# Entering a deformable round of a MetaFormer kernel, ScalarE copies the first image's turned hats before it takes the second image's absolute distances

## The chip, the cores and the metric

The kernel runs on one core of a Trainium2 chip. The metric is the device time of one execution in microseconds (us); lower is better. Five engines work side by side, each on its own list of instructions, and meet at semaphores: TensorE (PE, with its weight loads shown apart as PEld), VectorE (DVE), ScalarE (ACT), GpSimd (POOL) and SyncE (SP), which only issues transfers here.

## The reference

The input is 8 images of 32 channels and 16 x 16 pixels, in float32. Eight stages follow each other, each with a residual and a normalisation: local attention, a top-2 mixture of experts, an L1-distance convolution, an expert-choice mixture, **two deformable convolutions**, another top-2 mixture, full attention with relative positions, another expert-choice mixture. The change lies in the deformable convolutions. Cut to what matters, with 4 groups and 9 taps:

```python
def _dcnv4(t, H, W, Wv, bv, Wom, bom, Wo):
    value = (t @ Wv + bv).reshape(N, H, W, G, Cg)
    om = (t @ Wom + bom).reshape(N, H, W, G, 3 * K)
    offset, mask = om[..., :2 * K].reshape(N, H, W, G, K, 2), om[..., 2 * K:]
    loc_y = ys + ky + offset[..., 1]
    loc_x = xs + kx + offset[..., 0]
    sampled = _bilinear_gather(value, loc_y, loc_x)
    out = (sampled * mask[..., None]).sum(axis=4)
    return out.reshape(N, L, C) @ Wo

t = _dcnv4(t, H, W, Wv, bv, Wom, bom, Wo)
y = jax.nn.relu(_bn(t, gamma, beta))
t = _dcnv4(y, H, W, Wv, bv, Wom, bom, Wo)
y = _bn(t, gamma, beta) + shortcut
```

## The kernel before, in words

All engines' programs are written out by hand; nothing is scheduled by a tool. A deformable convolution is a round, `turn` 0 and then `turn` 1, and each round is the function `deform` of every engine. Its unit of work is half an image (128 of the 256 pixels, one per partition), numbered n = 2b + half, 16 units per round. The diff's "first image" and "second image" are units n = 0 and n = 1, the two halves of image b = 0. The bilinear weights are "hats", relu(1 - |distance|), in x and in y.

One unit passes through the engines in this order:

- **GpSimd, `distances`** (lines 246 and 249): subtracts pixel coordinates from the sampling points, into DXY. It signals `dxy_ready`.
- **ScalarE, `absolute`** (line 472): |DXY| in place, for 1476 columns. **ScalarE, `hats`** (line 482): relu(1 - |DXY|) into HXY, again 1476 columns. It signals `hxy_ready`.
- **GpSimd, `masked`** (line 258): y hats times the mask, into HYM (`hym_ready`).
- **TensorE, `turn_hats`** (line 1143): nine transposes of the x hats, in three groups of three, into banks 0 and 1 of PSUM in turn (`hx_turned`). A group may be written when its bank has been copied out.
- **ScalarE, `turned`** (line 491): three copies, one per group, of 384 columns each, into HXT (`hxt_ready`).
- **TensorE, `products`** (line 1162): nine matmuls, one per tap (two passes each in float32), into six banks in rotation (`prod_done`).
- **VectorE, `sample`** (line 816): nine multiplications by HYM, into PRD (`prod_used`).
- **GpSimd, `pairs`** (line 315): adds three taps' products to three others, once six of the nine are there. **VectorE, `sums`** (line 825): reduces the rest.

DXY, HXY, HXT, HYM and PRD have two slots each, one per half. In the trace DXY, HXY and HXT are parts of one buffer and all read as RINGS.

After the entry, TensorE interleaves the next unit's transposes between the present unit's products: group 0 ahead of the third product, group 1 ahead of the sixth, group 2 ahead of the ninth. So after unit 0's three groups and its first two products, TensorE waits for unit 1's hats.

At the entry VectorE prepares what the units need: `offsets` (line 781), `points` (lines 793 to 797) for units 0, 2, 4, 6, then 1, 3, 5, 7, then all eight units of the second half of the batch, and `values` (line 803) twice. Only after the last `values` does it start `sample`. GpSimd's order at the entry is: distances of units 0 and 1, masked of unit 0, distances of unit 2, **masked of unit 1**, distances of unit 3, pairs of unit 0, and then for each unit masked, distances, pairs.

Of the kernel before, what the change touches and what calls it, by code (L numbers as in the profile page):

```python
# [83 lines left out]
def metaformer(nc, x_in, cst_in, wa_in, wb_in, wc_in, wd_in, out):  # L84
# [3 lines left out]
    with ExitStack() as ctx:  # L88
# [7 lines left out]
        def view(t, col, dims, p0=0, n=P):  # L96

            if isinstance(t, tuple):
                t, first = t
                col = first + col  # L100
            w = t.shape[1]
            return bass.AP(t, p0 * w + col, [[w, n]] + [list(d) for d in dims])
# [49 lines left out]
        def cv(name, n, c=0, p0=0, np_=P):  # L152
            return cst[p0:p0 + np_, CST[name] + c:CST[name] + c + n]
# [48 lines left out]
        def after(eng, s, value):  # L202

            if not isinstance(value, int) or value > 0:
                eng.wait_ge(s, value)
# [139 lines left out]
        def _(act):  # L345
            tables = [0]

            def table(func):

                act.activation(spare[:, tables[0]:tables[0] + 1], cv("one", 1), func)  # L350
                tables[0] += 1
# [116 lines left out]
            def absolute(turn, b, half):  # L468
                n = 2 * b + half
                o = half * HATS  # L470
                act.wait_ge(dxy_ready, 16 * turn + n + 1)
                act.activation(view(DXY, o, [[1, HATS]]), view(DXY, o, [[1, HATS]]), ACT.Abs).then_inc(abs_done, 1)  # L472

            def hats(turn, b, half, begun=False):
                n = 2 * b + half
                o = half * HATS
                if not begun:
                    absolute(turn, b, half)
                act.wait_ge(abs_done, 16 * turn + n + 1)
                after(act, hx_turned, 3 * (16 * turn + n - 1))  # L480
                after(act, hym_ready, 16 * turn + n - 1)
                act.activation(view(HXY, o, [[1, HATS]]), view(DXY, o, [[1, HATS]]), ACT.Relu, scale=-1.0,  # L482
                               bias=cv("one", 1)).then_inc(hxy_ready, 1)

            def turned(turn, b, half):
                n = 2 * b + half
                after(act, prod_done, 9 * (16 * turn + n - 1))
                for g in range(3):
                    act.wait_ge(hx_turned, 3 * (16 * turn + n) + g + 1)
                    o = (half * K9 + 3 * g) * P  # L490
                    act.activation(view(HXT, o, [[1, 3 * P]]), bank[(3 * half + g) % 2][:, 0:3 * P], ACT.Copy).then_inc(hxt_ready, 1)  # L491

            def deform(turn, src, src_ready, count):
                act.wait_ge(src_ready, count)
                after(act, val_done, NBH * turn)
                for bh in range(NBH):
                    act.activation(view(XW, bh * NR * NA * WW, [[NA * WW, NR], [WW, NA], [1, WW]]),
                                   view(src, bh * NPIX, [[WW, NR], [7 * WW, NA], [1, WW]]), ACT.Copy).then_inc(xw_ready, 1)
                hats(turn, 0, 0)
                absolute(turn, 0, 1)  # L500
                turned(turn, 0, 0)
                hats(turn, 0, 1, begun=True)

                def body(b, first=False):
                    for half in range(2):
                        if not (first and half == 0):
                            turned(turn, b, half)
                        hats(turn, b + 1, half)
                body(0, first=True)
                with act.Fori(1, B - 1) as b:  # L510
                    body(b)
                for half in range(2):
                    turned(turn, B - 1, half)
                act.wait_ge(smp_turned, turn + 1)
                act.activation(YC[:, :], bank[0][:, :], ACT.Copy, accum_out=c2[:, 3:4]).then_inc(sc_ready, 1)
                act.wait_ge(mean_ready, turn + 1)
                act.activation(D2[:, :], bank[1][:, :], ACT.Square, bias=c1[:, 0:1], accum_out=c2[:, 0:1]).then_inc(sq_ready, 1)
                table(ACT.Sqrt)
                act.wait_ge(bnv_ready, turn + 1)
                act.activation(c2[:, 1:2], c2[:, 2:3], ACT.Sqrt).then_inc(bsd_ready, 1)  # L520
                act.wait_ge(bn_ready, turn + 1)
                if turn == 0:
                    act.activation(YC[:, :], ACC[:, :], ACT.Relu, scale=c1[:, 2:3],
                                   bias=wc[:, WC["beta"]:WC["beta"] + 1]).then_inc(dc_ready, 1)

            act.wait_ge(wc_s, 16)
            deform(0, XNC, xnc_ready, 4)
            deform(1, YC, dc_ready, 1)
            norm(5, "eps5", then=ACT.Exp)
            top2(1)  # L530
# [846 lines left out]
```

## Time and profile before

| | us |
|---|---|
| median of three runs | 527.92 |
| lowest and highest of them | 526.73, 528.42 |
| the profiled execution, as timed | 528.59 |
| its span in the trace | 526.8 |
| turn 0's entry, first distances to the first pairs | 184.76 to 200.74 |
| turn 1's entry, the same | 296.62 to 312.58 |

The span is what the trace covers; 1.8 us of the execution's time lie around it. In the trace all times are from the span's start. Rows of the timeline give an instruction's (or a run of like instructions') start, its duration, engine, line of the kernel, output and inputs, and in brackets how long the engine had been idle before it and what ended that. Everything that the change can touch directly lies in the two entries, about 16 us each.

### The profile page before, as it was taken

To read this page: it belongs to the slowest core of one execution; us is meant where nothing else is said; L and a number is where in the kernel's file an instruction comes from. 1 tells how busy PE (TensorE), PEld (TensorE's weight loads), DVE (VectorE), ACT (ScalarE), POOL (GpSimd) and SP (SyncE) were. 2 spreads that over 40 slices of the span, in tenths; PEclk is the share of its full clock that TensorE was granted. 3 is DMA by queue.
4 is the path that set the end of the run, shared out by engine and by line. 5 is a ranking of instruction groups with operands and counts; after the bars stand their busy time and mean duration, and the time that the engine had idled before them with its cause. 6 is when DMAs were issued, how large, how long until landed. Compare 5 with 4: busy or idle time off the path is not lost.

```text
span 526.8 us, 10309 instructions
## 1 busy us (share of the span) xinstructions
PE 479.0 (91%) x3346; PEld 344.6 (65%) x3346; DVE 427.1 (81%) x1015; ACT 303.1 (58%) x554; POOL 212.6 (40%) x168
## 2 busy tenths in 40 slices
PE   6979899999987759999999689999998999999785
PEld 6868533332356637777777467777777897777574
DVE  4978899998772598999997799999995787888541
ACT  2742448898735268777760487777721228777340
POOL 4004450000000089999973389999942040000000
PEclk9999999999998779999999979999999999999895
DMA  8700000000000000000000000000000000000000
GB/s 323 318 1 1 1 1 1 1 1 0 1 1 1 0 2 2 1 0 0 1 1 0 2 0 2 0 0 0 0 1 1 1 0 2 0 3 1 1 2 20
DMA packets 1476, 9.16 MB, mean 17 GB/s; under 512 B 160, under 2 KB 928, under 8 KB 1056
## 3 DMA queue, kind: packets, MB, share of 16 engines
q1 hardware_dynamic: 1296, 8.62, 4.1%
q8 instruction: 22, 0.36, 0.3%
q14 instruction: 14, 0.11, 0.1%
q10 hardware_dynamic: 144, 0.07, 0.0%
HBM read 8.43 MB, written 0.26 MB: 16 GB/s over the span
## 4 chain that ended last, share of the span: by engine, by line
PE 66%; DVE 18%; issue 6%; ACT 4%; POOL 4%; DMA 0%; DVEq 0%; SPq 0%; POOLq 0%
PE bank L1162 24%; PE bank L1107 12%; PE bank L1143 6%; PE bank L965 6%; PE bank L921 4%; PE bank L974 3%; DVE RINGS L746 2%; PE bank L1112 2%; PE bank L987 2%; POOL RINGS L246 1%; DVE SM L619 1%; POOL PR L267 1%; DVE SMT L825 1%; DVE PR L658 1%; DVE PRD L816 1%
## 5 line engine op out<-in xcount | busy, mean ns | idle before, releaser
L1162 PE MATMUL bank<-VB,RINGS 128*128 (+1 forms) x576 | 158.1, 412 | 0.3
L246 POOL TENSOR_TENSOR RINGS<-LXA,cst 128x1152 f32<-128x1152 f32 x32 | 68.9, 2153 | 126.4 <-DVE LXA L797 126.4
L1162 PEld LDWEIGHTS bank<-VB,RINGS 128*128 128x128 f32 x576 | 103.3, 193 | 22.7 <-issue 2.1
L816 DVE TENSOR_TENSOR PRD<-bank,HYM 128x288 f32<-128x288 f32 x288 | 110.4, 449 | 7.4 <-PE bank L1162 2.7
L746 DVE TENSOR_SCALAR RINGS<-XP,wb 128x512 f32<-128x512 f32 x176 | 79.4, 527 | 7.9 <-PE bank L1107 6.6
L921 PE MATMUL bank<-cst 128*128 128x128 f32 x650 | 80.4, 285 | 0.0
L451 ACT ACTIVATE RINGS<-XP,wb 128x512 f32<-128x512 f32 x112 | 70.1, 715 | 16.9 <-PE bank L1107 16.8
L921 PEld LDWEIGHTS bank<-cst 128*128 128x128 f32 x650 | 79.3, 201 | 0.5
L1107 PE MATMUL bank<-RINGS,cst 128*32 128x512 f32 x576 | 74.5, 600 | 3.6 <-DVE RINGS L746 3.4
L315 POOL TENSOR_TENSOR PRD<-PRD 128x864 f32<-128x864 f32 x32 | 65.0, 2031 | 16.3 <-DVE PRD L816 16.3
L825 DVE TENSOR_REDUCE SMT<-PRD 128x1728 f32 (+1 forms) x32 | 62.2, 1943 | 0.1
L1143 PE MATMUL bank<-cst,RINGS 128*128 128x128 f32 x288 | 50.0, 286 | 11.7 <-ACT RINGS L482 8.6
L472 ACT ACTIVATE RINGS<-RINGS 128x1476 f32<-128x1476 f32 x32 | 45.8, 1432 | 23.9 <-POOL RINGS L249 23.7
L491 ACT ACTIVATE RINGS<-bank 128x384 f32<-128x384 f32 x96 | 43.2, 481 | 28.1 <-PE bank L1143 28.1
L1107 PEld LDWEIGHTS bank<-RINGS,cst 128*32 128x32 f32 x576 | 22.9, 110 | 53.5 <-issue 26.6
L1143 PEld LDWEIGHTS bank<-cst,RINGS 128*128 128x128 f32 x288 | 37.5, 146 | 30.1 <-ACT RINGS L482 10.6
L482 ACT ACTIVATE RINGS<-RINGS,cst 128x1476 f32<-128x1476 f32 x32 | 48.9, 1528 | 4.4 <-ACT RINGS L472 4.2
L391 ACT ACTIVATE SM<-SM,nm 128x256 f32<-128x256 f32 x80 | 40.0, 500 | 13.9 <-DVE nm L619 13.9
L965 PE MATMUL bank<-RINGS,QC 128*128 128x256 f32 x160 | 40.8, 383 | 0.0
L267 POOL TENSOR_TENSOR PR<-PR 128x256 f32<-128x256 f32 x16 | 11.5, 728 | 65.2 <-DVE PR L658 65.2
L625 DVE COPY RINGS<-bank 128x512 f32<-128x512 f32 x40 | 27.5, 691 | 9.0 <-PE bank L974 9.0
L357 ACT ACTIVATE sd<-var,cst 128x8 f32<-128x8 f32 x16 | 4.8, 301 | 50.5 <-DVE var L573 50.3
(235 smaller groups left out, 537.9 us busy)
## 6 DMA issues: line engine op xcount, KB each, us to landing
wb<-in_wb SPq DMA_DIRECT2D x1, 3068.5 KB, 12.5
wd<-in_wd SPq DMA_DIRECT2D x1, 2729.5 KB, 21.0
wc<-in_wc SPq DMA_DIRECT2D x1, 1255.0 KB, 15.0
cst<-in_cst SPq DMA_DIRECT2D x1, 645.0 KB, 5.5
XC<-in_x SPq DMA_DIRECT2D x2, 128.0 KB, 2.4
out_y<-XC SPq DMA_DIRECT2D x2, 128.0 KB, 1.8
wa<-in_wa SPq DMA_DIRECT2D x1, 209.0 KB, 5.7
cst<-in_cst ACTq DMA_DIRECT2D x1, 66.0 KB, 2.6
```

The lines of the kernel that those rows point to most:

```text
L246: pool.tensor_tensor(view(DXY, o, [[WW, KG * NA], [1, WW]]), view(LXA, n * KG * NA, [[1, KG * NA], [0, WW]]), view(cst, CST["xg"], [[0, KG ...
L315: pool.tensor_tensor(second, second, first, ALU.add).then_inc(paired, 1)
L451: act.activation(view(RINGS, slot, [[NPIX, NBH], [WW, HH], [1, WW]]), view(XP, tap // 3 * PADW + tap % 3, [[PADW * PADW, NBH], [PADW, HH], ...
L482: act.activation(view(HXY, o, [[1, HATS]]), view(DXY, o, [[1, HATS]]), ACT.Relu, scale=-1.0, bias=cv("one", 1)).then_inc(hxy_ready, 1)
L746: dve.tensor_scalar(view(RINGS, (k % DRING) * F, [[NPIX, NBH], [WW, HH], [1, WW]]), view(XP, tap // 3 * PADW + tap % 3, [[PADW * PADW, NBH ...
L816: dve.tensor_tensor(view(PRD, (half * K9 + k) * 288, [[72, G], [NR, CG], [1, NR]]), view(bank[2 + (9 * half + k) % LOOK], 0, [[72, G], [NR ...
L825: dve.tensor_reduce(view(SMT, bh * NPIX + half * P + (b - B4 * bh) * C, [[1, C]]), view(PRD, (half * K9 + PAIRS) * 288, [[NR, C], [288, K9 ...
L921: pe.matmul(bk[:, 0:P], ident, ident, start=True, stop=True)
L965: ins = pe.matmul(scores_bank[s % 3][:, j * 256:j * 256 + 256], QC[:, q0:q0 + P], view(KM, b * NPIX, [[1, NPIX]]), start=True, stop=True)
L1107: pe.matmul(bank[2][32 * j:32 * j + 32, :], cv(rep, 32, 28 - 4 * i), RINGS[:, slot:slot + F], start=(i == 0 and tap == TAPS[0]), stop=(i = ...
L1143: ins = pe.transpose(bk[:, k * P:(k + 1) * P], view(HXY, at, [[1, P]]), ident)
L1162: pe.matmul(bank[2 + (9 * half + k) % LOOK][:, 0:288], view(HXT, (half * K9 + k) * P, [[1, P]]), view(VB, b * 288, [[1, 288]]), start=True ...
```

## The change

In `deform`, ScalarE took the absolute distances of unit 1 (`absolute(turn, 0, 1)`) before it copied unit 0's transposed hats (`turned(turn, 0, 0)`), and then ran `hats` of unit 1 without its first part. Now it copies first, and `hats` of unit 1 takes the absolute distances itself, as for all other units. Nothing else moves; the same instructions are issued.

```diff
-            def hats(turn, b, half, begun=False):
+            def hats(turn, b, half):
                 n = 2 * b + half
                 o = half * HATS
-                if not begun:
-                    absolute(turn, b, half)
+                absolute(turn, b, half)
                 act.wait_ge(abs_done, 16 * turn + n + 1)
...
                 hats(turn, 0, 0)
-                absolute(turn, 0, 1)
                 turned(turn, 0, 0)
-                hats(turn, 0, 1, begun=True)
+                hats(turn, 0, 1)
```

ScalarE's order at the entry of turn 0, in the kernel before. L497 prepares the windows for the values, L472 is `absolute`, L482 the relu of `hats`, L491 a copy of `turned` (from bank0 or bank1):

```order
L497 ACTIVATE PRD<-XNC 128x288
L472 ACTIVATE RINGS<-RINGS 128x1476 [waits dxy_ready]
L482 ACTIVATE RINGS<-RINGS,cst 128x1476 [waits abs_done]
L472 ACTIVATE RINGS<-RINGS 128x1476 [waits dxy_ready]
L491 ACTIVATE RINGS<-bank0 128x384 [waits hx_turned]
L491 ACTIVATE RINGS<-bank1 128x384 [waits hx_turned]
L491 ACTIVATE RINGS<-bank0 128x384 [waits hx_turned]
L482 ACTIVATE RINGS<-RINGS,cst 128x1476 [waits abs_done]
L472 ACTIVATE RINGS<-RINGS 128x1476 [waits dxy_ready]
```

The same place in the changed kernel, whose line numbers are one lower from `hats` on (L481 for L482, L490 for L491):

```order
L496 ACTIVATE PRD<-XNC 128x288
L472 ACTIVATE RINGS<-RINGS 128x1476 [waits dxy_ready]
L481 ACTIVATE RINGS<-RINGS,cst 128x1476 [waits abs_done]
L490 ACTIVATE RINGS<-bank0 128x384 [waits hx_turned]
L490 ACTIVATE RINGS<-bank1 128x384 [waits hx_turned]
L490 ACTIVATE RINGS<-bank0 128x384 [waits hx_turned]
L472 ACTIVATE RINGS<-RINGS 128x1476 [waits dxy_ready]
L481 ACTIVATE RINGS<-RINGS,cst 128x1476 [waits abs_done]
L472 ACTIVATE RINGS<-RINGS 128x1476 [waits dxy_ready]
```

The second L472 (unit 1) has moved from ahead of the three copies to behind them, directly ahead of its own relu.

TensorE's order at the same place, which is the same before and after but for line numbers; the first nine transposes (L1143) are unit 0's, the first two L1162 its first two products, and the transposes behind them are unit 1's group 0:

```order
L1143 MATMUL bank0<-cst,RINGS 128x128 [waits hxy_ready]
L1143 MATMUL bank0<-cst,RINGS 128x128 x2
L1143 MATMUL bank1<-cst,RINGS 128x128 x3
L1143 MATMUL bank0<-cst,RINGS 128x128 [waits hxt_ready]
L1143 MATMUL bank0<-cst,RINGS 128x128 x2
L1162 MATMUL bank2<-VB,RINGS 128x288 [waits val_used,om_used,hxt_ready]
L1162 MATMUL bank3<-VB,RINGS 128x288 [waits om_used]
L1143 MATMUL bank1<-cst,RINGS 128x128 [waits hxt_ready,hxy_ready]
```

Nothing moved here: the third group of transposes waits for the first copy, and the last row for unit 1's relu.

## Rows read from the trace of the kernel before

**Rows 1.** The page: busy time by engine, and the chain that ended last.

```profile
PE 479.0 (91%) x3346; PEld 344.6 (65%) x3346; DVE 427.1 (81%) x1015; ACT 303.1 (58%) x554; POOL 212.6 (40%) x168
PE 66%; DVE 18%; issue 6%; ACT 4%; POOL 4%; DMA 0%; DVEq 0%; SPq 0%; POOLq 0%
```

**Rows 2.** Timeline of ScalarE, turn 0's entry.

```profile
187.68 1.43 ACT L472 ACTIVATE RINGS<-RINGS 128x1476 f32<-128x1476 f32 x1 [5.39 <-POOL RINGS L249]
189.15 1.53 ACT L482 ACTIVATE RINGS<-RINGS,cst 128x1476 f32<-128x1476 f32 x1
191.64 1.43 ACT L472 ACTIVATE RINGS<-RINGS 128x1476 f32<-128x1476 f32 x1 [0.96 <-POOL RINGS L249]
192.98 0.85 ACT L491 ACTIVATE RINGS<-bank 128x384 f32<-128x384 f32 x2
194.44 0.49 ACT L491 ACTIVATE RINGS<-bank 128x384 f32<-128x384 f32 x1 [0.61 <-PE bank L1143]
194.83 1.52 ACT L482 ACTIVATE RINGS<-RINGS,cst 128x1476 f32<-128x1476 f32 x1
```

**Rows 3.** Timeline of TensorE, turn 0's entry.

```profile
190.73 1.54 PE L1143 MATMUL bank<-cst,RINGS 128*128 128x128 f32 x6 [4.31 <-ACT RINGS L482]
193.50 0.90 PE L1143 MATMUL bank<-cst,RINGS 128*128 128x128 f32 x3 [1.23 <-ACT RINGS L491]
...
196.40 0.90 PE L1143 MATMUL bank<-cst,RINGS 128*128 128x128 f32 x3
...
198.63 0.49 PE L1143 MATMUL bank<-cst,RINGS 128*128 128x128 f32 x3
198.96 1.62 PE L1162 MATMUL bank<-VB,RINGS 128*128 128x288 f32 x6
```

**Rows 4.** Timeline of GpSimd, turn 0's entry and end.

```profile
192.27 2.21 POOL L246 TENSOR_TENSOR RINGS<-LXA,cst 128x1152 f32<-128x1152 f32 x1
...
196.42 0.77 POOL L258 TENSOR_TENSOR HYM<-RINGS,OM 128x324 f32<-128x324 f32 x1 [0.99 <-ACT RINGS L482]
...
200.74 2.03 POOL L315 TENSOR_TENSOR PRD<-PRD 128x864 f32<-128x864 f32 x1 [0.70 <-DVE PRD L816]
...
206.28 2.03 POOL L315 TENSOR_TENSOR PRD<-PRD 128x864 f32<-128x864 f32 x1
...
271.26 2.02 POOL L315 TENSOR_TENSOR PRD<-PRD 128x864 f32<-128x864 f32 x1 [1.30 <-DVE PRD L816]
```

**Rows 5.** Busy time by stretch: PE, PEld, DVE, ACT, POOL (instructions), granted clock.

```profile
200.74:269.95 69.21, 69.21 (x347) 54.01 (x346) 65.94 (x126) 53.08 (x63) 69.21 (x50) 1.00 0.00 0
```

**Rows 6.** Timeline of VectorE, turn 0's entry.

```profile
192.51 2.29 DVE L794 SCALAR_TENSOR_TENSOR LXA<-BX,OM 128x288 f32<-128x288 f32 x1
...
195.78 0.31 DVE L796 TENSOR_SCALAR BX<-BX 128x288 f32<-128x288 f32 x1
196.12 0.46 DVE L797 SCALAR_TENSOR_TENSOR LXA<-BX,OM 128x288 f32<-128x288 f32 x1
196.50 1.85 DVE L803 TENSOR_TENSOR VB<-bank,wc 32x288 f32<-32x288 f32 x4
198.38 4.48 DVE L816 TENSOR_TENSOR PRD<-bank,HYM 128x288 f32<-128x288 f32 x11
```

**Rows 7.** Timeline of turn 1's entry, several engines.

```profile
302.58 1.12 PE L1143 MATMUL bank<-cst,RINGS 128*128 128x128 f32 x6 [4.31 <-ACT RINGS L482]
...
306.68 1.52 ACT L482 ACTIVATE RINGS<-RINGS,cst 128x1476 f32<-128x1476 f32 x1
...
307.63 0.31 DVE L796 TENSOR_SCALAR BX<-BX 128x288 f32<-128x288 f32 x1
307.97 0.46 DVE L797 SCALAR_TENSOR_TENSOR LXA<-BX,OM 128x288 f32<-128x288 f32 x1
...
323.85 2.03 POOL L315 TENSOR_TENSOR PRD<-PRD 128x864 f32<-128x864 f32 x1 [0.16 <-DVE PRD L816]
```

**Rows 8.** Timeline of TensorE in turn 1, the sixth product.

```profile
311.20 1.62 PE L1162 MATMUL bank<-VB,RINGS 128*128 128x288 f32 x6
```

**Rows 9.** Busy time by half microsecond, columns as in group 5.

```profile
190.50:191.00 0.50, 0.27 (x2) 0.28 (x3) 0.50 (x1) 0.17 (x1) 0.50 (x2) 0.50 0.00 0
303.00:303.50 0.50, 0.50 (x5) 0.29 (x2) 0.50 (x1) 0.01 (x1) 0.50 (x2) 0.56 0.00 0
```

## The prediction

> **What bounds the kernel now.** I read the page first: TensorE is busy for 91% of the span and carries 66% of the chain that ended last, GpSimd 4% [rows 1]. Taken alone this says that whatever lets TensorE start a round earlier shortens it. The timeline of the two rounds says otherwise. From the first pairs at 200.74 to 269.95 GpSimd is busy for 69.21 of 69.21 us [rows 5], and its next idle time is the 1.30 us that end at 271.26 [rows 4]. It takes 206.28 - 200.74 = 5.54 us per unit. TensorE is as full in this stretch [rows 5], because it only follows: its own rate comes from three transposes and three products, and those begin 198.96 - 198.63 = 0.33 us apart, then 1.62 less an overlap of 0.16 for six passes, so about 1.78 us a third and 5.35 us a unit. GpSimd is slower by 0.19 us a unit. Over the round's dozen units TensorE uses up a lead of over 2 us and ends tied to GpSimd, which feeds it through the distances. So a round's end is set by when GpSimd starts its unbroken run at the first pairs, not by TensorE's first product.
>
> What lets that run start? In turn 0 GpSimd had been idle for 0.70 us when VectorE's sixth product released it at 200.74 [rows 4]. VectorE began its products at 198.38, straight after `values`, and does eleven in 4.48 us without a gap, 0.41 each: six end at 200.8 [rows 6]. So the entry is set by VectorE's serial preparation, lines 794 to 803, and neither ScalarE nor TensorE is in it. The slack of the others against it: unit 1's masked on GpSimd may come 0.70 us later before it moves the first pairs, and TensorE's sixth product starts at 198.96 [rows 3] while VectorE wants it at 198.38 + 5 x 0.41 = 200.4.
>
> TensorE has less slack further on. The two entries are the same schedule, 111.85 us apart (unit 1's relu starts at 194.83 and at 306.68, line 797 at 196.12 and at 307.97 [rows 2, 6, 7]). But in turn 1 the sixth product starts at 311.20 [rows 8], 0.39 us later than 198.96 + 111.85, and there GpSimd waits 0.16 us for VectorE at the third pairs, 323.85 [rows 7]; in turn 0 it does not. So TensorE can be 0.39 - 0.16 = 0.23 us later than in turn 0 for nothing, and beyond that each microsecond counts.
>
> **The change part by part.** No instruction is added or removed; per turn one of 1.43 us moves behind three copies. DMAs, SyncE's queue and GpSimd's order stay. Turn 0, worked from rows:
>
> - Unit 0's relu ends at 190.68 and TensorE starts at 190.73. Three transposes at the half clock take 0.90 us [rows 3], so group 0 is there at 191.63. Before, ScalarE was then in unit 1's absolute, which had waited for GpSimd until 191.64 and let the first copy start at 192.98 [rows 2]. Now the copy starts at 191.67 (0.04 from 194.40 to the copy at 194.44), 1.31 us earlier.
> - It lasts 0.49 and releases group 2 at 192.19, where it was 193.50. Group 2 ends 0.90 later, at 193.09, and its copy starts at 193.13. The distances that unit 1's absolute needs have been there since 191.64, so it starts 0.39 after the last copy (194.83 - 194.44), at 193.52.
> - A relu follows its absolute by 189.15 - 187.68 = 1.47 us. So unit 1's relu starts at 194.99; before it was 194.83 [rows 2]. The reorder fills 1.31 us early and pays 1.47 back on the way: **+0.16 us** for unit 1's hats in turn 0.
> - That delay is hidden twice: masked of unit 1 moves from 196.42 to 196.58, inside GpSimd's 0.70 us, and TensorE's transposes from 196.40 to 196.56, inside the 0.23 us. If that cover were gone it would cost 0.16. Term of turn 0: **0**.
>
> [...] Term of turn 1: **-0.16**.
>
> The clock may help besides. In the entries TensorE now goes from group 1 to group 2 and the first two products with hardly a gap, where it idled 1.23 us before [rows 3], so its clock may come back earlier. No row shows how much earlier; worth at most the distance to the bound, it moves only TensorE and is worth nothing once GpSimd's 0.16 us are gone. I take 0.
>
> Sum: 528.59 of the profiled execution becomes 528.43. That execution lies 0.67 above the median of the runs shown, so against the median, 527.92 - 0.16 = **527.8 us**.
>
> **What speaks against it: VectorE and GpSimd take turns.** Line 794 took 2.29 us from 192.51 to 194.80, the like line 797 0.46 [rows 6]: GpSimd's distances held 192.27 to 194.48 [rows 4], and line 794 ended 0.32 after them. So one of lines 793 to 797 that comes upon a running GpSimd instruction waits it out. [...]
>
> [...]
>
> **The rivals.**
>
> - **Masked overtakes line 797 or 796 (the slower side).** If masked starts before line 797, it holds 0.75 us and line 797 ends 0.32 later: 307.95 + 0.75 + 0.32 = 309.02, not 308.43, so +0.6 us on `values`, VectorE's products and the first pairs. In both turns 1.2 less 0.16: about 529.0. If it starts before line 796 (307.63), line 796 goes after masked and line 797 then finds unit 3's distances running: 307.63 + 0.75 + 2.2 + 0.32 = 310.9, +2.5 us a turn, both turns 527.9 + 5.0 = 532.9, one turn 530.4. [...] Where the clock falls relative to the entry differs already between the two turns, so it can differ between executions. [...] For the small form 0.12, for the large 0.07.
> - **TensorE is the bound after all (the faster side).** Then what counts is when the sixth product starts, and it waits for the second `values`, done at 196.50 + 1.85 = 198.35 [rows 6], and 111.85 later, at 310.20, in turn 1. At most 198.96 - 198.35 = 0.6 and 311.20 - 310.20 = 1.0 us are to be had, 1.6 in all: 526.3. It needs the clock back early in both turns, and 69.21 busy us of GpSimd out of 69.21 speak against it. 0.06.
> - **The delay is not hidden.** If the turn's slack is smaller than I read, turn 0 pays its 0.16, and in both turns with the lower clock throughout 0.32: 528.2. 0.05.
>
> The forecast itself keeps 0.70.
>
> **How the numbers follow.** About 1.6 us, 0.3%, is what a measurement of this kernel can tell from no change; the three runs lie 1.7 us apart. Forecast, hidden delay lost and small lock all lie within it: 0.87. The large lock is slower by more: 0.07, and with the spread of runs 0.08. The faster rival reaches the limit just: 0.05 with the spread. The range takes in the faster bound (526.3) and the small lock with 0.4 us of spread (529.4); it leaves out the large lock and the tails of the runs' spread.
>
> **What the profile after would show.** First copy at about 1.0 us after unit 0's relu ends in turn 0 (before: 2.30); unit 1's absolute behind the three copies; its relu 0.16 us later in turn 0 and about 0.25 earlier in turn 1 against relu 0, depending on the clock at groups 0 and 2; the first pairs still 16.0 us after the first distances in both turns; no idle time of GpSimd before the third pairs of turn 1; line 797 still at 0.46 us. I would be wrong if line 796 or 797 grows to 1 us or more and the first pairs come later with it, or if GpSimd's run shows gaps and the round ends with TensorE's start.

## The result, and the profile after

| | before | after |
|---|---|---|
| median of 20 runs each, us | 527.83 | 529.47 |
| lowest, highest | 526.43, 529.45 | 527.95, 530.34 |
| span of the profiled execution | 526.8 | 528.0 |
| first pairs after the first distances, turn 0 / turn 1 | 15.98 / 15.96 | 17.09 / 16.80 |
| third pairs after the first pairs | 11.08 / 11.27 | 11.42 / 11.42 |

The ratio is 1.0025, 95% interval 1.0014 to 1.0036: the change makes the kernel slower by 0.25%, about 1.3 us. That is the distance of the means, 527.75 and 529.07 us; the medians lie 1.64 us apart, because the runs fall into groups: those of after are eight from 527.95 to 528.22 and twelve from 529.24 to 530.34.

ScalarE's timeline of after, turn 0 (it answers to [rows 2]):

```profile
188.90 1.53 ACT L481 ACTIVATE RINGS<-RINGS,cst 128x1476 f32<-128x1476 f32 x1
191.42 1.13 ACT L490 ACTIVATE RINGS<-bank 128x384 f32<-128x384 f32 x2 [0.99 <-PE bank L1141]
192.90 0.49 ACT L490 ACTIVATE RINGS<-bank 128x384 f32<-128x384 f32 x1 [0.35 <-PE bank L1141]
193.29 1.43 ACT L472 ACTIVATE RINGS<-RINGS 128x1476 f32<-128x1476 f32 x1
194.75 1.53 ACT L481 ACTIVATE RINGS<-RINGS,cst 128x1476 f32<-128x1476 f32 x1
```

Unit 1's relu starts 4.32 us after unit 0's has ended (190.43). It was 4.15 before, and the prediction had 194.99 - 190.68 = 4.31. The reorder did what its arithmetic said. TensorE in the same stretch (to [rows 3]):

```profile
190.48 2.38 PE L1141 MATMUL bank<-cst,RINGS 128*128 128x128 f32 x9 [4.30 <-ACT RINGS L481]
192.66 2.13 PE L1160 MATMUL bank<-VB,RINGS 128*128 128x288 f32 x4
196.32 0.90 PE L1141 MATMUL bank<-cst,RINGS 128*128 128x128 f32 x3 [1.54 <-ACT RINGS L481]
197.02 3.08 PE L1160 MATMUL bank<-VB,RINGS 128*128 128x288 f32 x6
199.90 0.65 PE L1141 MATMUL bank<-cst,RINGS 128*128 128x128 f32 x3
200.38 1.62 PE L1160 MATMUL bank<-VB,RINGS 128*128 128x288 f32 x6
```

The 1.23 us of idle time ahead of unit 0's third group are gone, and 1.54 us stand ahead of unit 1's transposes, where there was nearly none. Two more rows of the kernel before, unit 0's first two products and its third to fifth, stand around the transposes of 196.40 in [rows 3]:

```profile
194.20 2.13 PE L1162 MATMUL bank<-VB,RINGS 128*128 128x288 f32 x4
...
197.09 1.70 PE L1162 MATMUL bank<-VB,RINGS 128*128 128x288 f32 x6
```

There TensorE goes from 194.20 on without a wait, and products 3 to 5 take 1.70 us. After the change they take 3.08 us, and the sixth starts at 200.38. Counted from TensorE's first transposes that is 9.90 us, where it was 198.96 - 190.73 = 8.23 [rows 3].

Busy time by half microsecond, columns as in [rows 5], the clock third from the end:

```profile
189.50:190.00 0.50, 0.00 (x0) 0.00 (x0) 0.49 (x2) 0.50 (x1) 0.50 (x1) 0.97 0.00 0
190.00:190.50 0.50, 0.02 (x1) 0.02 (x1) 0.47 (x2) 0.43 (x1) 0.50 (x1) 0.50 0.00 0
199.50:200.00 0.50, 0.50 (x3) 0.25 (x2) 0.18 (x1) 0.03 (x1) 0.44 (x1) 0.50 0.00 0
200.00:200.50 0.50, 0.50 (x5) 0.50 (x4) 0.36 (x1) 0.00 (x0) 0.00 (x0) 0.79 0.00 0
```

The granted clock is at its lower level (0.50) from 190.0 to 200.2, 10.2 us; before it was from 190.5 to 197.2, 6.8 us. VectorE and GpSimd show what that costs (to [rows 6] and [rows 4]); VectorE first, then GpSimd:

```profile
195.88 0.46 DVE L795 SCALAR_TENSOR_TENSOR LXA<-BX,OM 128x288 f32<-128x288 f32 x1
196.25 1.85 DVE L801 TENSOR_TENSOR VB<-bank,wc 32x288 f32<-32x288 f32 x4
198.13 1.55 DVE L814 TENSOR_TENSOR PRD<-bank,HYM 128x288 f32<-128x288 f32 x4
200.14 0.46 DVE L814 TENSOR_TENSOR PRD<-bank,HYM 128x288 f32<-128x288 f32 x1 [0.46 <-PE bank L1160]
201.07 1.43 DVE L814 TENSOR_TENSOR PRD<-bank,HYM 128x288 f32<-128x288 f32 x3 [0.47 <-PE bank L1160]
```

```profile
201.61 2.02 POOL L315 TENSOR_TENSOR PRD<-PRD 128x864 f32<-128x864 f32 x1 [1.67 <-DVE PRD L814]
...
213.03 2.03 POOL L315 TENSOR_TENSOR PRD<-PRD 128x864 f32<-128x864 f32 x1 [0.31 <-DVE PRD L814]
...
297.81 2.15 POOL L246 TENSOR_TENSOR RINGS<-LXA,cst 128x1152 f32<-128x1152 f32 x1 [12.55 <-DVE LXA L795]
```

VectorE's preparation is as before (line 795 at 0.46 us), and its products start on time, but from the fifth on they wait for TensorE. The sixth comes late, GpSimd idles 1.67 us instead of 0.70 ahead of the first pairs and 0.31 ahead of the third. Turn 0, from its first distances to those of turn 1, takes 297.81 - 184.52 = 113.29 us; it was 296.62 - 184.76 = 111.86. That is +1.43. The first pairs account for 1.11 of it, and up to the third pairs 0.34 more come in (1.45 in all, by rows rounded to 0.01). Turn 1, from its first distances to the start of its last sums (397.05 before, 399.15 after), takes 101.34 instead of 100.43, +0.91. The rest of this one execution was 1.1 us shorter than in the profile before, in code that the change does not touch.

### The profile page after: what moved, and what is told of

Same layout as the page of the kernel before. It is cut to its first block, busy times and chain, and to the rows that moved or that the text cites. A ratio compares the mean times of both kernels' runs of the same rounds, so it can differ in the third digit from the quotient of the medians.

```text
span 528.0 us, 10309 instructions
## 1 busy us (share of the span) xinstructions
PE 480.5 (91%) x3346; PEld 345.1 (65%) x3346; DVE 427.4 (81%) x1015; ACT 303.8 (58%) x554; POOL 212.4 (40%) x168
## 4 chain that ended last, share of the span: by engine, by line
PE 67%; DVE 18%; issue 6%; ACT 5%; POOL 3%; DMA 0%; DVEq 0%; SPq 0%; POOLq 0%
PE bank L1160 25%; PE bank L1105 12%; PE bank L1141 7%; PE bank L963 6%; PE bank L919 3%; PE bank L972 3%; DVE RINGS L744 2%; PE bank L1110 2%; PE bank L985 2%; ACT RINGS L481 1%; DVE SM L617 1%; POOL PR L267 1%; DVE SMT L823 1%; DVE PR L656 1%; ACT RINGS L472 1%
## 5 line engine op out<-in xcount | busy, mean ns | idle before, releaser
L1160 PE MATMUL bank<-VB,RINGS 128*128 (+1 forms) x576 | 160.2, 416 | 0.3
L1160 PEld LDWEIGHTS bank<-VB,RINGS 128*128 128x128 f32 x576 | 104.4, 195 | 23.1 <-issue 1.9
L919 PE MATMUL bank<-cst 128*128 128x128 f32 x650 | 79.1, 282 | 0.0
L919 PEld LDWEIGHTS bank<-cst 128*128 128x128 f32 x650 | 78.1, 199 | 0.5
L490 ACT ACTIVATE RINGS<-bank 128x384 f32<-128x384 f32 x96 | 43.7, 483 | 33.0 <-PE bank L1141 32.8
L472 ACT ACTIVATE RINGS<-RINGS 128x1476 f32<-128x1476 f32 x32 | 45.8, 1431 | 20.8 <-POOL RINGS L249 20.6
L481 ACT ACTIVATE RINGS<-RINGS,cst 128x1476 f32<-128x1476 f32 x32 | 48.9, 1529 | 4.4 <-ACT RINGS L472 4.2
L267 POOL TENSOR_TENSOR PR<-PR 128x256 f32<-128x256 f32 x16 | 11.5, 726 | 66.0 <-DVE PR L656 66.0
```

The lines of the kernel that those rows point to most:

```text
L919: pe.matmul(bk[:, 0:P], ident, ident, start=True, stop=True)
L1160: pe.matmul(bank[2 + (9 * half + k) % LOOK][:, 0:288], view(HXT, (half * K9 + k) * P, [[1, P]]), view(VB, b * 288, [[1, 288]]), start=True ...
```

## The experiments

Theory A: the new idle gap of TensorE ahead of unit 1's transposes keeps its clock low, and products at half the clock are late for VectorE. Theory B: the new order itself delays unit 1. Theory C: the two profiles differ by chance. Beside them stands the prediction's slower rival, called the lock from here on: a step of VectorE that comes upon a running GpSimd instruction waits it out, as line 794 did with 2.29 us against line 797's 0.46 [rows 6]. The prediction's small and large lock are the two forms of that rival, the last step alone and both.

**Gap filled.** The changed kernel with three dummy matmuls in the gap (`keep_warm`; nobody reads their results).

```diff
                 for k in range(K9):
+                    if first and k == 2:
+                        keep_warm(bank[4], 3)
                     if more and k in TURN_AT:
```

> The changed kernel, with three dummy matmuls (128 columns each, results never read) on TensorE between unit 0's second product and unit 1's first transposes, in both turns; in the profile after TensorE idles 1.54 us there and the clock stays at its lower level for 10.2 us, against 6.8 us before. Theory A (the new gap keeps the clock low): three dummies at the half clock take about 1.3 of the 1.54 us, the clock is back about 3.4 us sooner in both turns, first pairs come 16.0 us after the first distances again and the time is that of the kernel before or up to 0.5 us less, ratio 0.998 to 1.001. Theory B (the new order itself delays unit 1): the dummies change nothing, first pairs stay 17.1 and 16.8 us after the first distances, ratio 1.002 to 1.004. Theory C (the clock's fall and return are chance, the profiles differ by luck): ratio stays near 1.0025 and the low stretch varies.

Median 526.60, ratio to the kernel before 0.9971 (0.9953 to 0.9989). The timeline of TensorE and GpSimd, turn 0 (line 919 is the dummies, and L1162 `products` here):

```profile
191.56 2.13 PE L1162 MATMUL bank<-VB,RINGS 128*128 128x288 f32 x4
...
193.48 1.30 PE L919 MATMUL bank<-cst 128*128 128x128 f32 x6
195.22 0.55 PE L1141 MATMUL bank<-cst,RINGS 128*128 128x128 f32 x3 [0.45 <-ACT RINGS L481]
...
195.61 1.62 PE L1162 MATMUL bank<-VB,RINGS 128*128 128x288 f32 x6
...
199.40 2.04 POOL L315 TENSOR_TENSOR PRD<-PRD 128x864 f32<-128x864 f32 x1 [0.54 <-DVE PRD L814]
```

Nothing of the order was undone, unit 1's hats come when they came after the change, and yet products 3 to 5 take 1.62 us and the first pairs come 15.98 and 15.96 us after the first distances. Theory B falls. The ratio is even somewhat below what A expected; what the two entries account for comes further down.

**The lower clock avoided, in both orders.** Seventeen dummies ahead of unit 0's first transposes, in the changed kernel and in the kernel before.

```diff
                     ins.then_inc(val_done, 1)
+                keep_warm(bank[1], 17)
                 turn_hats(turn, 0, 0)
```

> The changed kernel, with 17 dummy matmuls on TensorE ahead of unit 0's first transposes in both turns, about 3.9 of the 4.3 us in which it idles there. Theory A: the clock never falls at the entries, products 3 to 6 run at the full clock and the penalty of 1.0 to 1.4 us a turn goes: ratio 0.996 to 0.999. But transposes at the full clock also bring unit 1's hats about 0.8 us sooner, so masked of unit 1 meets VectorE's lines 794 and 795; if it locks them out, line 795 takes 1 us or more and 0.3 to 2.5 us a turn are lost: ratio 0.999 to 1.008, and the profile must show it. Theory B: unit 1's delay comes from the order, the ratio stays at 1.002 or above with line 795 at 0.46 us.

> The kernel before, with the same 17 dummy matmuls ahead of unit 0's first transposes in both turns. Theory A: here the lower clock costs little, since the sixth product is in time but for the 0.16 us of turn 1; ratio 0.997 to 1.000, and the difference between the two orders falls from 1.3 us to within 0.5 us of each other with the clock kept up. Theory B: the difference between the orders stays at 1.3 us.

Changed kernel 526.89, ratio 0.9987 (0.9975 to 1.0000); kernel before 527.28, ratio 0.9995 (0.9976 to 1.0013). The orders no longer differ by 1.3 us; if anything the new one is ahead. Both show the lock. VectorE and GpSimd in the kernel before with dummies, turn 0:

```profile
194.43 0.31 DVE L796 TENSOR_SCALAR BX<-BX 128x288 f32<-128x288 f32 x1
194.73 0.74 POOL L258 TENSOR_TENSOR HYM<-RINGS,OM 128x324 f32<-128x324 f32 x1 [0.65 <-ACT RINGS L482]
194.77 1.01 DVE L797 SCALAR_TENSOR_TENSOR LXA<-BX,OM 128x288 f32<-128x288 f32 x1
195.43 2.36 POOL L246 TENSOR_TENSOR RINGS<-LXA,cst 128x1152 f32<-128x1152 f32 x1
195.71 1.85 DVE L803 TENSOR_TENSOR VB<-bank,wc 32x288 f32<-32x288 f32 x4
```

Masked of unit 1 started 0.04 us ahead of line 797, which then took 1.01 and not 0.46 us; the first pairs came at 16.54 and 16.52 us. In the changed kernel line 795 took 0.90 us, with the pairs at 16.41. In its profile the clock, up at the start of the entry, fell at 12.2 and 12.5 us, after the gap, which without the lower clock is 2.49 us long in turn 0.

**New order in turn 0 alone.**

```diff
-                absolute(turn, 0, 1)
+                if turn == 1:
+                    absolute(turn, 0, 1)
                 turned(turn, 0, 0)
-                hats(turn, 0, 1, begun=True)
+                hats(turn, 0, 1, begun=turn == 1)
```

> The new order in turn 0 alone, turn 1 as before. From the profiles turn 0 lost 1.43 us and turn 1 0.91 us, and the rest of the program happened to be 0.9 us shorter. Theory A: the penalty is each turn's own, so this kernel loses about half of the 1.3 us, ratio 1.001 to 1.002; in its profile turn 0 has the long low stretch (about 10 us) and turn 1 the short one (about 7 us). Theory C (chance): no relation to the turn.

Ratio 1.0000 (0.9981 to 1.0020): the interval holds both half of the loss and nothing, so the time tells nothing. (In the two first profiles the rest of the program differed by 1.1 us, not by the 0.9 of the expectation.) The profile is as A has it: turn 0 with the clock back at 15.5 us and pairs at 16.99, turn 1 with 11.5 and 15.97.

**The old gap filled.** The kernel before, with dummies in its own 1.23 us. The added wait keeps them from writing into bank 2 before VectorE has read it.

```diff
-                turn_hats(turn, 0, 0)
+                turn_hats(turn, 0, 0, (0, 1))
+                pe.wait_ge(om_used, 4 * turn + 1)
+                keep_warm(bank[2], 2)
+                turn_hats(turn, 0, 0, (2,))
```

> The kernel before, with two dummy matmuls on TensorE in the 1.23 us in which it idles ahead of unit 0's third group of transposes, in both turns. Theory A (idle gaps of TensorE inside the entry decide when its clock comes back): the low stretch is 6.8 us or shorter in both turns, the 0.16 us of GpSimd at the third pairs of turn 1 go, and the time falls by 0.2 to 1.5 us, ratio 0.997 to 0.9995; it depends on how often the kernel before has the long stretch of about 10 us in runs that were not profiled. Theory B (the gain of the filled gap came from the new order together with the dummies): no change, 0.9995 to 1.001.

Ratio 0.9977 (0.9962 to 0.9992), median 526.65. The one profile shows no difference to the first one of the kernel before in its entries (clock back at 12.4 and 13.2 us, pairs at 15.96 and 15.95). A second profile of the kernel before, below, has the clock back only at 14.6 us and pairs at 16.44; if the dummies take such entries away, that would be the gain, but no run shows it.

**A third order**, to bring masked onto VectorE's steps on purpose.

```diff
-                turned(turn, 0, 0)
-                hats(turn, 0, 1)
+                turned(turn, 0, 0, (0,))
+                absolute(turn, 0, 1)
+                turned(turn, 0, 0, (1, 2))
+                hats(turn, 0, 1, begun=True)
```

> A third order: copy of group 0, then unit 1's absolute, then the copies of groups 1 and 2, then its relu, in both turns. From rows at the half clock unit 1's relu ends at 5.0 us after unit 0's, 0.65 us sooner than in the kernel before, and masked of unit 1 starts at 5.1 us, where VectorE's line 794 to 796 (the scalar step ahead of the last one) starts at 5.1. Theory L (VectorE and GpSimd take turns, the first holds): if masked is first, VectorE's last two steps end 2.5 us later and the first pairs come 18.4 us after the first distances, ratio 1.008; if second, the last step alone takes 0.9 to 1.0 us and the pairs come at 16.4 to 16.6, ratio 0.999 to 1.003. Theory N (they do not block each other): pairs at 16.0, ratio 0.998 to 1.000.

Median 533.97, ratio 1.0092 (1.0062 to 1.0121). Of the six runs two took 529.2 and 529.9 us and four 533.9 to 534.8; the profile is of the first. VectorE and GpSimd, turn 0 (L797 is here what line 796 was, L798 what 797 was):

```profile
193.88 0.75 POOL L258 TENSOR_TENSOR HYM<-RINGS,OM 128x324 f32<-128x324 f32 x1 [0.30 <-ACT RINGS L482]
193.92 0.87 DVE L797 TENSOR_SCALAR BX<-BX 128x288 f32<-128x288 f32 x1
...
194.58 2.21 POOL L246 TENSOR_TENSOR RINGS<-LXA,cst 128x1152 f32<-128x1152 f32 x1
194.83 2.29 DVE L798 SCALAR_TENSOR_TENSOR LXA<-BX,OM 128x288 f32<-128x288 f32 x1
...
201.27 2.03 POOL L315 TENSOR_TENSOR PRD<-PRD 128x864 f32<-128x864 f32 x1 [3.53 <-DVE PRD L817]
```

Masked was first by 0.04 us, then unit 3's distances were ahead of the last step: 2.29 us. First pairs at 18.35 us, +2.4. In turn 1 of the same profile masked was 0.06 us later, only the last step was caught (0.90 us), and the pairs came at 16.39. Theory L holds. The four longer runs would fit the large form in both turns, but none of them has a kept trace.

This profile also bears on the clock. In turn 0 it fell at 5.2 us and was back at 15.4, as late as in the new order, although TensorE's gap ahead of unit 1's transposes is only 0.68 us long here. So the runs don't say how long a gap has to be.

**More profiles of the unchanged kernels and of the filled gap.**

> The kernel before, unchanged, profiled once more. Theory A: the low stretch at the entries is mostly 6.8 us, the first pairs 16.0 us after the first distances. Theory C (chance): it may as well be 10.2 us, with the pairs at 17.

> The changed kernel, unchanged, profiled once more. Theory A: the low stretch is again about 10 us in at least one of the turns, the first pairs at 16.8 to 17.1 us. Theory C: as likely 6.8 us and 16.0.

> The changed kernel with the gap of 1.54 us filled by three dummies, profiled once more. Clock theory: whenever the clock falls, it is back by 13.3 us after the first distances and the first pairs come at 16.0; a return at 14.6 or later, with pairs at 16.4 to 17.1, would say that the gap is not what keeps it low.

> The changed kernel, unchanged, profiled a third time. Clock theory: the clock is back only at 15.0 to 16.0 us after the first distances in both turns, first pairs at 16.8 to 17.1, as in three of the four entries seen so far and, after a second fall, in the fourth.

The two entries of each of these profiles, and of the profiles above that keep one of these orders and have no dummies ahead of it, in us after the first distances (fall and return of the clock read in stretches of 0.1 us):

| entry | clock falls | is back | first pairs | third after first |
|---|---|---|---|---|
| old order, first profile | 5.7 / 6.4 | 12.5 / 13.3 | 15.98 / 15.96 | 11.08 / 11.27 |
| old order, second profile | 4.3 / 4.3 | 14.6 / 14.6 | 16.44 / 16.45 | 11.41 / 11.42 |
| old order, turn 1 beside the new one | 4.7 | 11.5 | 15.97 | 11.09 |
| new order, first profile | 5.5 / 4.8 | 15.7 / 15.0 | 17.09 / 16.80 | 11.42 / 11.42 |
| new order, second profile | 5.8 / 5.3 | 16.0 / 15.6 | 16.88 / 17.07 | 11.41 / 11.43 |
| new order, third profile | 6.0 / 6.9 | 9.4 / 10.3 | 15.96 / 15.97 | 11.06 / 11.05 |
| new order, turn 0 alone | 5.2 | 15.5 | 16.99 | 11.42 |
| new order, gap filled | 4.2 / 5.0 | 11.0 / 11.8 | 15.98 / 15.96 | 11.07 / 11.06 |
| new order, gap filled, second profile | 5.3 / 6.2 | 12.2 / 9.6 | 15.96 / 15.96 | 11.08 / 11.07 |

In the entry whose clock fell at 5.8 it was back at 9.2, fell again at 12.6 and came back for good at 16.0. Chance does play a part (theory C): where the clock falls differs between executions, and the expectation that the third profile would repeat the others was wrong; that execution took 527.33 us. But at falls of 4.8 to 5.8 us all five entries of the new order have the clock back for good only at 15.0 or later, while those of the filled gap, at 4.2 to 5.3, are back by 12.2. So in these entries it is the gap that holds the clock down. The old order's gap can do it too: where the clock fell at 4.3, it was back at 14.6, and where it fell at 4.7 or later, at 11.5 to 13.3. The half-microsecond rows of the second profile of the changed kernel, turn 0, show a fall behind the gap:

```profile
194.00:194.50 0.50, 0.50 (x3) 0.08 (x1) 0.50 (x1) 0.50 (x1) 0.50 (x2) 1.00 0.00 0
...
197.00:197.50 0.50, 0.50 (x4) 0.34 (x4) 0.49 (x2) 0.50 (x1) 0.50 (x2) 0.86 0.00 0
197.50:198.00 0.50, 0.50 (x3) 0.36 (x2) 0.49 (x2) 0.47 (x2) 0.50 (x1) 0.50 0.00 0
```

The clock came back at 193.95, in the midst of unit 0's first two products (192.88 to 194.54). TensorE then idled for 2.00 us until 196.55, and at 197.35 the clock was down again, in the midst of work. Between the entries of the table the first fall lies anywhere from 4.2 to 6.9 us after the first distances.

The third profile of the changed kernel, where the clock came back ahead of the gap and stayed, by the timeline of TensorE and GpSimd in turn 0:

```profile
196.38 0.55 PE L1141 MATMUL bank<-cst,RINGS 128*128 128x128 f32 x3 [1.88 <-ACT RINGS L481]
...
196.77 1.62 PE L1160 MATMUL bank<-VB,RINGS 128*128 128x288 f32 x6
...
200.56 2.03 POOL L315 TENSOR_TENSOR PRD<-PRD 128x864 f32<-128x864 f32 x1 [0.55 <-DVE PRD L814]
```

The gap is there, 1.88 us long, the products run at the full clock (1.62 us for three), and GpSimd idles 0.55 us, not 1.67.

Averages over the table give a check of size: the seven entries of the new order without dummies have their third pairs at 28.00 us after the first distances, the five of the old at 27.41. Two turns of 0.58 us are 1.2 us, against 1.3 measured; with so few entries that is an agreement in size and no more.

The two rounds taken whole, from turn 0's first distances to the start of turn 1's last sums, say it more plainly:

| profiles | the two rounds, us | the rest of the span, us |
|---|---|---|
| old order | 212.3, 213.6 | 314.5, 312.4 |
| new order | 214.6, 214.7, 211.9 | 313.4, 313.3, 313.6 |
| new order, gap filled | 212.1, 212.0 | 311.6, 314.0 |

The rounds are long where the clock comes back late, and 212 us where it does not. The rest, which no edit touches, varies by 2.9 us all the same. So the groups among the runs of one kernel aren't shown to come from the entries, and a ratio alone can't be read down to a few tenths of a us: the filled gap measures 1.5 us faster than the kernel before, and the rounds account for about 0.9 of that.

**Clock held up and lock taken away, in both orders.** The dummies of the two warm kernels, nine more in the changed one's gap, and one wait on GpSimd:

```diff
                 masked(turn, 0, 0)
                 distances(turn, 1, 0)
+                pool.wait_ge(lxa_ready, 3 * turn + 3)
                 body(0, 2)
```

> The changed kernel with all idle time of TensorE in the entries filled (17 dummies ahead of unit 0's transposes, 9 between unit 0's second product and unit 1's transposes), and with one wait more on GpSimd: masked of unit 1 waits until VectorE has ended its last preparation step (line 795). Clock theory plus lock theory: the clock stays up through both entries, line 795 is back at 0.46 us, first pairs 16.0 us after the first distances, third pairs 11.1 later, ratio to the kernel before 0.996 to 0.999, and equal to the next kernel within 0.1%. Order theory (the new order costs something of its own): 0.5 us or more slower than the next kernel.

> The kernel before with the 17 dummies ahead of unit 0's first transposes and the same wait of GpSimd. Clock stays up, line 797 at 0.46 us where it took 1.01 with the dummies alone, first pairs at 16.0 instead of 16.5 us, ratio 0.996 to 0.999. If the lock is not what cost the 0.5 us, pairs stay at 16.5.

Changed kernel 526.52, ratio 0.9983 (0.9966 to 0.9999); kernel before 526.54, ratio 0.9989 (0.9974 to 1.0004). The two ratios are the same within 0.1%, though their intervals alone would leave room for 0.2%. The two rounds take 212.0 us in both profiles. VectorE and GpSimd in the kernel before, held, turn 0:

```profile
194.72 0.46 DVE L798 SCALAR_TENSOR_TENSOR LXA<-BX,OM 128x288 f32<-128x288 f32 x1
...
195.26 0.75 POOL L258 TENSOR_TENSOR HYM<-RINGS,OM 128x324 f32<-128x324 f32 x1 [1.24 <-DVE LXA L798]
...
199.33 2.04 POOL L315 TENSOR_TENSOR PRD<-PRD 128x864 f32<-128x864 f32 x1 [0.49 <-DVE PRD L817]
```

The last step is back at 0.46 us and the pairs at 15.98, so the 0.5 us of the warm kernels were the lock's. In this kernel's turn 1 the clock still fell, from 8.6 to 12.0 us, at no cost. The runs of both kernels still lie in groups, at about 525.4, 526.5 and 527.9 us.

## Why the prediction was wrong

**What held.** GpSimd's first pairs set the end of a round: +1.11 and +0.34 us there make up the turn's +1.43. The new order costs unit 1's hats what I had worked out for the half clock: they come 4.32 us after unit 0's, forecast 4.31, before 4.15. That alone is hidden, as turn 0 of the third profile shows, with masked at 11.81 us and pairs at 15.96. Line 795 stayed at 0.46 us in all six profiled entries of the changed kernel, so the slower rival was not what happened. Its prices were right where it was made to happen: 0.6 us forecast and 0.41 to 0.56 measured for the last step alone, 2.5 and 2.4 for both.

**The step that failed** is "The clock may help besides ... I take 0". I had seen that TensorE would run from group 1 into the products without a gap, and took this for a clock that returns sooner or at the same time. I had not followed the gap to where it went: two products end at 194.8, unit 1's relu at 196.3, so 1.54 us of idle time stand there, where TensorE of the kernel before was busy until the clock was back. The term I set to 0, with a gain as its other end, measured 1.11 + 0.34 us in turn 0 and 0.84 + 0.15 in turn 1. Of the prediction's two signs of being wrong the second came: GpSimd's run has a gap, 0.31 us ahead of the third pairs. The long stretch isn't the new order's alone: the second profile of the kernel before has it, and its first pairs come 0.46 us later for it. In the third profile of the changed kernel the clock did return sooner (9.4 and 10.3 us), which is the case I had in mind. At the first pairs it was worth nothing, as I wrote; at turn 1's third pairs GpSimd's 0.16 us were gone.

**The slack.** I set 0.23 us of free delay for TensorE from two entries with returns at 12.5 and 13.3 us and then asked only whether a delay of 0.16 fits. The question was what a later return costs: a product of two passes takes about 1.03 us at the lower level (3.08 for three) and 0.49 to 0.54 at the upper one (1.62 for three, 1.46 less the overlap of 0.16), and the three ahead of the sixth product took 3.08 instead of 1.62 us: 1.46 us, six times that slack.

**Turn 1's term of -0.16 us** has no run that shows it. In the kernel before TensorE's first six transposes take 1.12 us in turn 1 and 1.54 in turn 0 [rows 7, 3], and the clock reads 0.56 over 303.0 to 303.5, after they had begun at 302.58 [rows 9, 7]. From that one execution I took group 0 of turn 1 at the full clock, 1.12 - 0.64 = 0.48 us, and so unit 1's relu 0.25 us sooner than 306.68, which would cover the 0.16 us of GpSimd at the third pairs. It would also bring masked of unit 1 to 308.02, only 0.05 us behind the start of line 797 at 307.97 [rows 7], which spoke for the slower rival (0.12 and 0.07). Behind it masked does no harm: in turn 0 of the kernel before it starts 0.30 us after line 797, which keeps its 0.46 us [rows 4, 6]. In the first profile after, the clock fell ahead of group 0 (at 4.8 us) and unit 1's relu came 4.38 us after unit 0's had ended instead of 4.15, 0.23 us later. In the third it fell at 6.9 us, the six transposes took 0.87 us, and the relu came after 4.02 us: 0.13 us sooner, not 0.25. The 0.16 us of GpSimd were gone there, but with the clock back 3.0 us sooner (10.3 instead of 13.3), so they can't be put down to the order. A term that hung on where the clock falls in one execution was no term.

**The chances.** Within 0.3% had 0.87, and 0.25% lies within; but the sign was wrong and the range ended at 529.4, just short of 529.47. No rival had a later return of the clock as its mechanism.

## What to carry to other kernels

When a reorder closes an idle gap of TensorE, find out where the gap goes, and what the products behind it cost if the clock is still at its lower level: here three took 3.08 us instead of 1.62, and VectorE waited 0.46 and 0.47 us for them. A few dummy matmuls in the gap (three here) are cheap: they turned a loss of 0.25% into a gain of 0.29% over the kernel before, and both orders end at the same time once the clock is held up and GpSimd is kept behind VectorE's preparation. Which of the two gaps, 1.2 us early or 1.5 us later, is the dearer one in general isn't shown: the clock fell at different places in the entries compared.

Where the clock's fall differs between executions (4.2 to 6.9 us here), one profile before and one after are two draws. Two or three of each, set side by side by the same quantity, show the spread.

Work that arrives earlier can be worse: with unit 1's hats 0.7 us sooner, GpSimd took the turn from VectorE by 0.04 us and the kernel lost 0.9%. One wait that keeps GpSimd behind VectorE's last preparation step cost nothing, since GpSimd had 0.5 us of slack there.

## What was not expected of the hardware

- In the new order's first profile a return of the clock at 15.7 instead of 15.0 us moved the first pairs from 16.80 to 17.09: 0.29 us for 0.7 us more of the lower clock.
- A difference of 0.04 to 0.06 us in the start of one GpSimd instruction (10.96 against 11.02 us after the first distances) decided 2.0 us of the first pairs (18.35 against 16.39) in one and the same execution.
- The clock fell at 197.35 while TensorE was in back-to-back products, 0.8 us after an idle gap of 2.0 us had ended.
- The kernel before has the slow entry too: in its second profile the pairs came at 16.44 and 16.45 us. Filling its gap with two dummies gave 0.23%, though the one profile of that kernel shows no difference to the first one of the kernel before. That the unprofiled runs split as the profiles do was not shown.
- With a gap of only 0.68 us ahead of unit 1's transposes (the third order, turn 0) the clock was down from 5.2 to 15.4 us, 10.2 us in all, as long as with the gap of 1.54 us.
